# Another order of the first loads, weights split in two parts, and unused TensorE products in a two-layer attention and expert kernel

## The reference

```python
xn = _layernorm(x)
x = x + _L0_attn_ref(xn, ...) + _L0_ffn_ref(xn, ...)
xn = _layernorm(x)
x = x + _L1_attn_ref(xn, ...) + _L1_ffn_ref(xn, ...)
```

## Time and profile before

| what | value |
|---|---|
| median of 3 runs | 905.72 us (903.52 to 910.97) |
| span of the profiled execution | 907.0 us, 22696 instructions |
| TensorE busy | 835.0 us (92%) |
| VectorE, ScalarE, POOL busy | 700.4, 580.7, 624.7 us |
| first transposes, first product of 512 columns | 10.47 us, 16.83 us |
| layer 0's experts begin | about 246 us |

### The profile page before, as it was taken

One profiled execution on the slowest core, in us unless ns is written; L12 is line 12 of the kernel. 1 busy time (PEld: TensorE's weight loads), 2 busy tenths in 40 slices (PEclk: granted clock), 3 DMA queues, 4 the chain that ended last, 5 costly groups with the idle time before them and its releaser, 6 DMA issues.

```text
span 907.0 us, 22696 instructions
## 1 busy us (share of the span) xinstructions
PE 835.0 (92%) x7975; PEld 744.3 (82%) x7975; DVE 700.4 (77%) x1809; ACT 580.7 (64%) x1187; POOL 624.7 (69%) x598
## 2 busy tenths in 40 slices
PE   3789999999899999998899899899899999999996
PEld 2678879889799998987666666566799999999996
DVE  6687877887476898898789998989766556657776
ACT  5766474444376677768977777665766666666660
POOL 4157676777403788876888888888877777777662
PEclk9999999999999999999999999999999999999998
DMA  9799997114738998882111111113856655578986
GB/s 261 220 378 361 359 358 272 48 53 134 261 109 268 308 304 276 275 264 86 41 44 39 39 38 39 46 41 91 310 175 189 201 179 174 189 238 266 293 255 205
DMA packets 131135, 174.30 MB, mean 192 GB/s; under 512 B 15824, under 2 KB 85968, under 8 KB 130768
## 3 DMA queue, kind: packets, MB, share of 16 engines
q1 hardware_dynamic: 96864, 124.43, 42.8%
q0 software_dynamic: 16640, 34.37, 12.0%
q10 hardware_dynamic: 17520, 14.06, 5.1%
HBM read 93.96 MB, written 80.97 MB: 193 GB/s over the span
## 4 chain that ended last, share of the span: by engine, by line
PE 56%; DVE 25%; POOL 6%; issue 6%; ACT 5%; DMA 2%; SPq 0%; DVEq 0%; ACTq 0%; POOLq 0%
PE pair L960 14%; PE pair L927 6%; PE pair L896 6%; PE pair L898 6%; PE pair L897 6%; POOL sent L2155 5%; PE pair L730 3%; DVE a_en L1684 3%; PE pair L817 2%; DVE X L1618 2%; DVE stats_t L1249 2%; PE pair L737 1%; PE pair L739 1%; PE pair L738 1%; DVE X L1709 1%
## 5 line engine op out<-in xcount | busy, mean ns | idle before, releaser
L2155 POOL DMA_INDIRECT sent<-a_rows,slot x224 | 225.4, 1006 | 76.2 <-issue 59.9
L2166 POOL DMA_INDIRECT ex_joined<-outs,slot x128 | 136.0, 1062 | 84.8 <-DMA outs<-ex_tile_out 47.6
L896 PE MATMUL pair<-ex_x_hi,ex_w_hi 128*128 128x256 f32 x497 | 147.0, 296 | 0.6 <-DVE X L1709 0.4
L897 PE MATMUL pair<-ex_x_lo,ex_w_hi 128*128 128x256 f32 x497 | 140.5, 283 | 0.0
L898 PE MATMUL pair<-ex_x_hi,ex_w_lo 128*128 128x256 f32 x497 | 140.5, 283 | 0.0
L2257 POOL DMA_INDIRECT back<-ex_tile_out,slot x104 | 114.0, 1096 | 36.9 <-issue 25.9
L960 PE MATMUL pair<-ex_down_all,ex_hid 128*128 x1136 | 133.3, 276 | 1.3 <-ACT ex_hid L1971 0.9
L960 PEld LDWEIGHTS pair<-ex_down_all,ex_hid 128*128 128x128 f32 x1136 | 129.7, 192 | 3.1 <-issue 3.1
L1971 ACT ACTIVATE ex_hid<-pair,ex_stage 128x256 f32<-128x256 f32 x284 | 107.7, 493 | 6.0 <-PE pair L898 3.4
L1845 ACT ACTIVATE ex_w_hi<-ex_stage 128x768 fp32r<-128x768 f32 (+1 forms) x72 | 67.5, 938 | 62.1 <-DMA ex_stage<-in_experts 61.5
L896 PEld LDWEIGHTS pair<-ex_x_hi,ex_w_hi 128*128 128x128 f32 x497 | 94.9, 191 | 1.2 <-issue 0.6
(11 more groups left out here) (260 smaller groups left out, 2063.7 us busy)
## 6 DMA issues: line engine op xcount, KB each, us to landing
outs<-v_heads SPq DMA_DIRECT2D x8, 4352.0 KB, 37.3
ex_stage<-in_experts SPq DMA_DIRECT2D x72, 322.0 KB, 3.6
ex_stage<-in_experts SPq DMA_DIRECT2D x72, 320.0 KB, 4.9
ex_tile_in<-sent SPq DMA_DIRECT2D x72, 128.0 KB
outs<-ex_tile_out SPq DMA_DIRECT2D x71, 128.0 KB
ex_joined<-back ACTq DMA_DIRECT2D x15, 512.0 KB, 5.2
ex_tile_in<-sent SPq DMA_DIRECT2D x54, 132.0 KB
X<-in_x SPq DMA_DIRECT2D x16, 256.0 KB, 5.3
```

The source lines that it names most:

```text
L896: pe.matmul(o[:, of_half], wh, x_hi[i % 2][:, of_half], start=True, stop=False)
L897: pe.matmul(o[:, of_half], wh, x_lo[i % 2][:, of_half], start=False, stop=False)
L2155: pool.indirect_dma_start(out=sent[layer], out_offset=bass.IndirectOffsetOnAxis(ap=slot_i[layer][k][:, s, j:j + 1], axis=0), in_=rows[laye ...
L2166: pool.indirect_dma_start(out=joined[g % NJOIN][:, j, k, :], out_offset=None, in_=outs, in_offset=bass.IndirectOffsetOnAxis(ap=slot_i[0][k ...
```

## The change

Six things are done, all in layer 0's beginning.

- ACT's queue: `w0` is loaded second, behind `consts`; then `cols`, `gates`, `bias_raw` and `pad_addresses`.
- TensorE: `keep_warm(n)` makes n products of `ones` by `ones` (f32, 128 columns) into a bank that nobody reads. 13 of them run as soon as group 0 of x has landed and `ones` is written, ahead of group 0's transposes; 5 run behind these.
- The transposes of group 1 move from ahead of the loop to behind the first `shared_up`; the wait for the small loads moves there too.
- The split of the weights is cut in two parts, columns 0 to 383 (q, k, v) and 384 to 1151 (shared gate and up), on ACT and on VectorE. Between the parts ACT copies and rounds the columns of group 0, and VectorE makes the statistics of group 3 and `xT_lo` of group 0. TensorE waits for the first part ahead of the queries, for the second ahead of the first shared gate.
- `constants_once` is cut into `columns_once` (what only needs short operations) and `biases_once` (the row of ones and the biases by token). The first runs behind the second part of the weights, the second behind the shifts of group 3. `consts_made` counts three: `ones`, columns, biases. ACT waits for 2 ahead of the loop, TensorE for 3 ahead of the first keys and values.
- The down weights are halved behind the biases (`halve_down0`); the first `output0` waits for that. On ACT, rows of group 1 are normalised behind the second part of the weights; the columns of group 1 and the rows of group 2 follow behind the first queries in the first step, and the columns of group 2 and the rows of group 3 behind the first tanh.

```diff
@@ tensor_program, output0 @@
                 else:
                     pe.wait_ge(xT_ready, GPS)
+                    pe.wait_ge(w0_lo_here, 3)
@@ tensor_program @@
+            def keep_warm(n):
+
+                for _ in range(n):
+                    pe.matmul(bank[7][:, 0:P], ones[:], ones[:], start=True, stop=True)
+
+            pe.wait_ge(consts_made, 1)
+            pe.wait_ge(x_dma[0], 16)
+            keep_warm(13)
             pe.wait_ge(const_dma, 16)
             transposes(0, 0, 0)
-            transposes(0, 1, 1)
-            pe.wait_ge(small_dma, NSMALL * 16)
-            pe.wait_ge(consts_made, 1)
+            keep_warm(5)
             pe.wait_ge(w0_lo_here, 1)
...
                     queries0(g)
+                    if step == LEAD:
+                        pe.wait_ge(w0_lo_here, 2)
                     shared_gate(g, 0)
                     shared_up(g, 0)
                 if step == LEAD:
+                    pe.wait_ge(small_dma, NSMALL * 16)
+                    transposes(0, 1, 1)
                     transposes(0, 2, 2)
                     logits(0, (0,), 6, 0)
                     logits(0, (1,), 6, 1)
                     transposes(0, 3, 7)
+                    pe.wait_ge(consts_made, 3)
                 if new:
                     keys_values0(g, 0)
@@ vector_program @@
+            dve.memset(ones[:], 1.0).then_inc(consts_made, 1)
             dve.memset(ones_bf[:], 1.0)
-            dve.memset(ones[:], 1.0)
...
-            def weights_once():
+            def weights_once(part):
+                a, b = ((0, 3 * C), (3 * C, SPLIT0))[part]
+                dve.wait_ge(w0_hi_here, part + 1)
+                dve.tensor_tensor(w0_lo[:, a:b], w0[:, a:b], w0_hi[:, a:b].bitcast(F32), ALU.subtract).then_inc(w0_lo_here, 1)
+
+            def halve_down0():
                 dve.wait_ge(weight0_dma, 16)
-                dve.tensor_scalar(w0[:, SD0:], w0[:, SD0:], 0.5, None, ALU.mult)
-                dve.wait_ge(w0_hi_here, 1)
-                dve.tensor_tensor(w0_lo[:], w0[:, 0:SPLIT0], w0_hi[:].bitcast(F32), ALU.subtract).then_inc(w0_lo_here, 1)
+                dve.tensor_scalar(w0[:, SD0:], w0[:, SD0:], 0.5, None, ALU.mult).then_inc(w0_lo_here, 1)
...
             shifts(0, 1)
-            constants_once()
+            weights_once(0)
+            statistics(0, 3)
+            split_columns(0)
+            weights_once(1)
+            columns_once()
             shifts(0, 2)
-            statistics(0, 3)
-            weights_once()
             shifts(0, 3)
-            split_columns(0)
+            biases_once()
+            halve_down0()
             for n in STATS[0][1]:
                 statistics(0, n)
@@ scalar_program @@
             act.dma_start(consts[:], t["consts"]).then_inc(const_dma, 16)
-            for dst, src in ((gates[:], t["gates"]), (cols[:], t["cols"]), (bias_raw[:], t["bias"]), (pad_addresses[:], t["pad_addresses"])):
+            act.dma_start(w0[:], t["w0"]).then_inc(weight0_dma, 16)
+            for dst, src in ((cols[:], t["cols"]), (gates[:], t["gates"]), (bias_raw[:], t["bias"]), (pad_addresses[:], t["pad_addresses"])):
                 act.dma_start(dst, src).then_inc(small_dma, 16)
-            act.dma_start(w0[:], t["w0"]).then_inc(weight0_dma, 16)
...
             normalise(0, 0)
-            normalise(0, 1)
+            act.wait_ge(weight0_dma, 16)
+            act.activation(w0_hi[:, 0:3 * C], w0[:, 0:3 * C], ACT.Copy).then_inc(w0_hi_here, 1)
             columns(0, 0, 0)
             round_columns(0)
-            act.wait_ge(weight0_dma, 16)
-            act.activation(w0_hi[:], w0[:, 0:SPLIT0], ACT.Copy).then_inc(w0_hi_here, 1)
-            normalise(0, 2)
-            columns(0, 1, 1)
-            act.wait_ge(consts_made, 1)
+            act.activation(w0_hi[:, 3 * C:SPLIT0], w0[:, 3 * C:SPLIT0], ACT.Copy).then_inc(w0_hi_here, 1)
+            normalise(0, 1)
+            act.wait_ge(consts_made, 2)
...
                 if step == LEAD:
-                    normalise(0, 3)
-                    columns(0, 2, 2)
+                    columns(0, 1, 1)
+                    normalise(0, 2)
                 if new:
                     shared_tanh(g, 0)
                 if step == LEAD:
+                    columns(0, 2, 2)
+                    normalise(0, 3)
                     columns(0, 3, 7)
```

More of the change, by code:

```diff
@@ L1424, in biases, with columns_once @@
                 return dve.scalar_tensor_tensor(bias[:, a:b], bias[:, a:b].bitcast(F32), const("row")[:, 0:1], bias_raw[:, a:b], ALU.mult, ALU.add)
-            def constants_once():
+            def columns_once():
                 dve.wait_ge(const_dma, 16)
@@ L1433, in constants_once, with biases_once @@
                 dve.tensor_scalar(bqk1p1[:], cols[:, 2:4], 1.0, None, ALU.add)
-                dve.tensor_scalar(bqk1neg[:], cols[:, 2:4], -1.0, None, ALU.mult)
+                dve.tensor_scalar(bqk1neg[:], cols[:, 2:4], -1.0, None, ALU.mult).then_inc(consts_made, 1)
+            def biases_once():
                 dve.tensor_scalar(ones_r[:], consts[:, 0:512], 0.0, 1.0, ALU.mult, ALU.add)
                 biases(0, 3 * C).then_inc(consts_made, 1)
-            def weights_once():
+            def weights_once(part):
[3 more added lines that the diff above has]
+            def halve_down0():
                 dve.wait_ge(weight0_dma, 16)
-                dve.tensor_scalar(w0[:, SD0:], w0[:, SD0:], 0.5, None, ALU.mult)
-                dve.wait_ge(w0_hi_here, 1)
-                dve.tensor_tensor(w0_lo[:], w0[:, 0:SPLIT0], w0_hi[:].bitcast(F32), ALU.subtract).then_inc(w0_lo_here, 1)
+                dve.tensor_scalar(w0[:, SD0:], w0[:, SD0:], 0.5, None, ALU.mult).then_inc(w0_lo_here, 1)
             def next_layer_once():
```

## The result

The changed kernel takes 913.13 us (median of 4 runs, 911.68 to 918.91); the kernel before, run beside it, 905.57 (903.52 to 910.97). The ratio is 1.0081 with a 95% interval of 1.0051 to 1.0111: 4.6 to 10.1 us slower, about 7.5. I had said 905.8, no change, with a range that ended at 909. The time lies outside that range, and where I had let a gain and a loss cancel, the kernel is slower by more than the noise.

A forecast was written before the change was run, and what follows sets the result against it. TensorE led the chain of waits (56%), and a shift in the first 26 us was carried undiminished to the end. A schedule gain of 2.1 us and a load delay of 2.2 gave +0.1: 905.8 us, range 902 to 909.

The forecast's parts named there:

- the case in which the later steps absorb the shift: Steps from 26 to 62 us absorb the start's shift: exactly 905.7 us; shares the forecast's chance of 0.5.
- group 0 landing 2.2 us late: Token loads at the start: the weights' earlier transfer delays group 0, and the whole schedule, by 2.2 us.
- the rate from 4.1 us on, 70 token packets per us: DMA queues: beside the weights, tokens get about 70 packets per us, 175 during the weights' 2.5 us.
- group 0 still landed at 5.6 us (then the gain stands): Sign of being wrong: group 0's tokens not delayed, so the schedule's gain is kept.
- a gain of 2.1 us at the last logits: First step: new order with unused products ends the logits at 24.3 instead of 26.36 us, before the load delay.
- ScalarE, released by the column constants at 14.8: First step: VectorE finishes the column constants at 14.8 us, before the load delay, and ScalarE starts the queries' relu and exp.
- The pause of 1.3 us should keep the level: TensorE between the last unused products (12.3 us) and first product (13.6): the upper clock level survives.
- the new chain: First step: ScalarE, with two groups of rows and two copies moved behind its release, limits the gain to 2.1 us.
- 26.5: End of the first step's last logits once the load delay is included, +0.1 us against before.
- I had 5.0: TensorE's start: 13 unused products, 26 instructions, 19 slow and 7 fast, take 5.0 us.
- The rival in which the clock comes too late for the first transposes: TensorE's clock does not rise before group 0's transposes: 3.8 us on top of +0.1, 909.6 us; chance 0.15.
- My slower rival: Clock still low at group 0's transposes, first product 1.4 us later, nine products 3.9 us: 909.6 us; chance 0.15.

The follow-up runs named there:

- e5: Changed kernel plus 12 more unused TensorE products behind the transposes of group 1, filling one pause; ratio to the kernel before 1.0023.
- e7: Kernel before plus unused TensorE products alone (13 and 16), loads and order as before; 903.21 us against 906.84, ratio 0.9962.
- e8: Kernel before plus unused products (13 and 11), pads cleared first, biases and halving later, weights' high part earlier; ratio 0.9974.
- e6: Changed kernel run again, unaltered, on another chip; ratio to the kernel before 1.0057.
- e2: Kernel before with nothing but the loads in the new order; ratio 1.0040.
- e1: Changed kernel with the loads in the order of before; ratio to the kernel before 1.0056.
- e9: Kernel before with only the new order of work and the weights in two parts; old loads, no unused products; ratio 1.0048.
- e4: Changed kernel with POOL's clearing of the pads moved to POOL's beginning; ratio to the kernel before 1.0053.
- e3: Changed kernel without its 18 unused products; ratio to the kernel before 1.0124.
- e11: Changed kernel with the old loads, pads cleared at POOL's beginning and TensorE's pauses filled (13, 13 and 11 unused products); ratio to the kernel before 0.9969.
- e12: Kernel before with the new loads and unused products (13 and 16), order of work as before; ratio 1.0033.
- e10: Changed kernel with 22 unused products at the start instead of 13, and 12 more behind the transposes of group 1; ratio to the kernel before 1.0027.

## Why the prediction was wrong, point by point

**The shape was right.** The edited stretch is the first 26 us, and what happens there is carried on. Over the 13 runs of the table the shift of the keys goes from -3.1 to +8.3 us and the ratio roughly follows it, from 0.9962 to 1.0124. In the profiles the shift can be followed to the last products of the edited stage, the down products of the shared expert, which begin at 241.21 us before and at 246.60 in after: +5.4, as at the keys. In e5, e7 and e8 it is the same to 0.1 us (+3.6, -1.9, -3.1); in e6 it grew from 7.7 to 9.3, and there the level fell once more, between 125 and 135 us. On the two slower chips such falls are frequent in the steady steps, and the comparison can't be made. So the case in which the later steps absorb the shift did not happen. Behind this stage the two profiles of the result come closer: 4.6 us apart at the first transposes of the experts (246.20 and 250.84), 3.1 at the end. The medians are 7.5 us apart (4.6 to 10.1), which holds the 5.4. The two profiled executions are no typical pair: after's took 1.4 us less than its median, and before's, if its time lies above its span by as much as after's (1.7 us, my estimate), about 3 us more than its own.

**The loads: the size right, the place wrong.** I had group 0 landing 2.2 us late. It landed 0.5 us early in after and was on time in the others with these loads (taken up at 4.99 to 5.72 us, against 5.70 before), and group 1 took the whole delay, 2.6 us. The term that failed is the rate from 4.1 us on, 70 token packets per us: between 4 and 5 us, with the weights already moving, the tokens' queue moved 200 to 428 packets, just the rest of group 0, and only then fell to 16 to 38. The shifts of group 0 wait for VectorE's statistics of group 1, so the rows came 2.14 us late, by luck my number. For the same reason my sign of being wrong, "group 0 still landed at 5.6 us (then the gain stands)", pointed the wrong way. Alone the loads cost 3.3 us of keys and a ratio of 1.0040 (e2), where the constants stand behind group 2. The packet counts of the earlier trace rows were the right rows; I failed to ask which group stands behind the one that is through.

The Trainium skill's rule on queues (DMA: Bandwidth & Descriptors, section Queues, rings and completion order) that I weighed against them says that an engine drains a whole packet of one queue before it turns to the other. Between 5 and 6 us 36 token packets went beside 60 rows of the weights, and group 0 had gone through whole ahead of them. That is neither the alternation that I took from my counts nor a full stop; counts for a microsecond can't show the order within one engine.

**The order of the work: wrong in sign.** I forecast a gain of 2.1 us at the last logits with the unused products; with them and the old loads it loses 4.2 us there and 6.0 at the keys (e1), without them 6.0 and 7.9 (e9). Two steps of the prediction failed.

*"ScalarE, released by the column constants at 14.8"* (17.0 with the delay). It was released at 18.5. I priced the constants at 0.5 us by the earlier trace rows; they took 2.2 us (16.26 to 18.48), because I moved them without looking at what POOL does at the new place. There POOL clears the pads for 1.86 us, and a cast and a copy on VectorE stood for as long. e4 shows it by taking the clearing away (0.23 us), and e3 by the late cast that ended with it. Before, this clearing had other work of VectorE beside it, subtractions and statistics, and no instruction was stretched:

```profile
15.46 1.85 POOL L2223 MEMSET a_pads<- 128x2112 f32 x1
```

The Trainium skill (SBUF — State Buffer, section Who interferes with whom) has the rule: VectorE and GpSimd share a pair of ports, which the first to come holds for a whole instruction; `copy`, `cast` and `tensor_scalar` can go into modes that need it, `tensor_tensor` with two inputs only collides with what GpSimd reads. By that rule the trace agrees: the cast and the copy took 1.97 and 1.84 us and the subtractions beside the same clearing before took no longer than without it (0.68 us for the low part of xT). I had not looked it up.

*"The pause of 1.3 us should keep the level"*, from one row with a pause of 1.76 us. I checked the pause that I had computed and not the ones that I had made: my own schedule had TensorE done with the transposes of group 1 at 16.2 and waiting until 18.4 for the rows of group 2, 2.2 us, and I wrote of ScalarE as "the new chain" without asking what its chain does to TensorE's clock. I put this pause at nothing. With POOL out of the way it is exactly there, 2.22 us in e4, and the level fell behind it. In after the pause was 3.05 us, and ten microseconds of continuous work then ran at 1.2 GHz, where before 4.2 us of such work had brought the upper level; I had no row for how long a low level lasts behind a pause. From the transposes of group 3 to the end of the logits went 6.05 us (24.83 to 30.88) where my schedule had 3.2. Here the sum closes: group 3 was transposed at 24.83 instead of my 23.3 (+1.5, the late release), the low level took 2.9 more, and 26.5 + 4.4 gives the 30.9. Filling the pause won 2.4 to 3.8 us of keys (e5), mending port, pauses and loads together 5.7 (e11 against after). What the clearing costs by itself is less sure: taking it away alone won 0.65 us of keys (e4).

**The unused products: right, and misplaced.** 26 instructions took 5.37 us (I had 5.0); over the profiles with this start it was 4.50 to 5.89. The rival in which the clock comes too late for the first transposes was real: in e11 it made them 1.1 us late. In after it could do no harm, since the rows came at 12.4 us, long after these products were done. On their own, in the old order, the unused products are worth 2.0 us of keys and a ratio of 0.9962 (e7). The change surrounds them with pauses.

**The rivals.** My slower rival was the clock, with a price (+3.8 us over the forecast, 909.6) not far from what the low level took at the last logits (2.9), but in the wrong place: I looked for it ahead of the first product and it came behind the ninth. The time was 913.13, beyond that rival too. It got 0.15. The other place was in my own numbers.

**What stays open.** What exactly makes the level fall. In the first 60 us of these profiles it fell after every pause of 1.99 us or more that began at the upper level (1.99 and 3.05 in after, 2.05 and 2.22 in e6, 2.34 and 2.22 in e1, 2.33 and 2.22 in e4, 2.22 in e3), always when TensorE was at work again. It fell after two pauses of 1.65 and 1.34 us in e12, but not after 1.68 and 1.30 in e5, and in e5 and e10 it fell later, after a pause of 0.76 us and the first logits. A pause of 1.6 to 1.8 us in the second step left it alone in all 14 profiles. e11, whose longest pause ahead of its last logits was 0.51 us, kept it. Two executions of one program differ (after and e6). A run that shortens the pauses alone, with the logits left out, would tell more; it wasn't made. Open too is how much of each effect one profile per version shows: the clock's course was read once for each.

## What to carry to other kernels

When work is moved on one engine, write down the idle times that this gives TensorE, all of them, and price what follows each at the lower clock; a start that is earlier by 1 to 2 us is worth nothing if a pause of 2 to 3 us stands behind it. When one load is moved ahead, ask of each group behind it what waits for it: here it was not the first group that came late but the second, and the first one's work stood behind that. Look at what the other engines do at the new place of a moved instruction, POOL beside VectorE's copies above all. A few unused products in a wait that exists anyway were the whole gain here (0.4%). By the end of the first step the old order was the better one to put them in (28.48 us against 30.20 in e11); by time the two can't be told apart.

## What the runs showed of the hardware

- The granted clock reads 1.00 ahead of its first recorded change even where products run at the lower level: in e9 it is 1.00 up to 72 us, while the products run at the lower level until 37.8 us and the 16 logit instructions take 3.25 us. The durations of known shapes have to be read, not that column.

```profile
24.00:34.00 10.00, 10.00 (x44) 9.52 (x44) 3.69 (x9) 4.63 (x13) 1.65 (x3) 1.00 0.76 205
```

- Logit products of 32 columns double as well at the lower level (3.25 against 1.72 us for 16 instructions), and they take as long as products of 128 columns (0.107 us each against 0.112).
- A copy of 128x8 elements on VectorE took 1.84 us beside a clearing of 128x2112 on POOL, and 0.16 us without it (e4). A cast that came 0.7 us after the clearing had begun was held for the rest of it (e3).
- A transfer with rows of 6.6 KB on one queue left 16 to 38 packets of 512 bytes per us to the other (eight profiles, 5 to 6 us), against 575 beside small transfers.
- TensorE came back to the upper level after 4.2 us of continuous work before, and only after 10 us in after and 15.7 us in e9 (22.1 to 37.8).
